# Graph layer with a feed-forward network on one core: 32x32 block transposes on VectorE in place of TensorE's, down products one tile later, zeros on ScalarE's queue

## The chip, the cores and the metric

The kernel runs on 1 core of one Trainium2 chip. The metric is the device time of one execution in microseconds. Before the change it is 1678.12 us, the median of three runs.

## The reference

2500 nodes with 1024 features, 42500 edges. `xn` is the layer norm of `x`.

```
x = x + segment_sum((xn @ W)[src] * edge_weight, dst) + mix(xn)
x = x + ffn(layernorm(x))

mix:  q, k = xn @ Wq.T + bq, xn @ Wk.T + bk     (16 heads of 64), each divided by its norm
      s = sum over the map of phi(q) * phi(k);  v = xn @ Wv.T + bv;  out = s * v / s
ffn:  gate = silu(bitlinear(x, w_gate)); up = bitlinear(x, w_up); bitlinear(gate * up, w_down)
      bitlinear: rows scaled to integers of -128..127 by their largest value,
                 weights to -1, 0, 1 by their mean absolute value, then x @ w.T  (inner size 512)
```

## The kernel before

Rows are handled in 20 tiles of 125. Each engine has a program written out by hand, and semaphores order them; the order on an engine is the order of its code. Products in near full precision split both operands into a high part (made by ScalarE) and a low part (made by VectorE) and take three matmuls, `product3` at L364. The stages follow each other on TensorE:

- Gram stage (to about 163 us): rows are normalised, transposed and stored to `xnT`, and TensorE makes products of all rows, `gram` at L1391. Meanwhile GpSimd writes zeros into a dense matrix, `A_dense`, one strip of 1.28 MB at a time.
- Weight stage (to 313): high and low parts of Wq and Wk (`high_of_weights`, `low_of_weights`), then `fold`, which makes the map weights.
- Map stage (to 546): `map_tile`, 48 matmuls per tile with TH and TL. VectorE's `ex` add at L1144 starts when TensorE has ended the tile. VectorE also works off the edges in pairs of columns, `edges`, after the numbers of EDGE_PLAN, and GpSimd adds them into the dense matrices by indirect DMAs, `scatter_pair`: the first 20 pairs (ALONE) into matrix 0, each after a strip of zeros of matrix 1, the rest in turn into both. In tiles 10 to 17 a block of 128 rows of Wv is transposed by TensorE (`transposes`, eight matmuls against `ident`), copied back by ScalarE (L848) and stored by SP (L522).
- Stage of W (to 769): `source_tile`, results S stay in SBUF.
- Value stage (to 992): the same with Wv in WH and WL. VectorE's four steps after a tile are in `stage4_tile` (L1173 to L1180). Tiles 6 to 17 also take a chunk of the feed-forward weights each: VectorE scales and rounds it, ScalarE makes bf16 of it (L884), TensorE transposes it (L1569), ScalarE copies it (L887), SP stores it to `ternary` (L600).
- Aggregation (to 1553): five groups of four output tiles (eight PSUM banks). For each of the 20 source tiles ScalarE makes SH and AH, VectorE adds the two loads of the dense matrices and makes SL and AL (`low_of_sources`), TensorE does 24 matmuls of 512 columns. There are two buffers of each, so ScalarE's copy waits until TensorE has released that buffer. Between the pairs of source tiles VectorE quantises the four tiles of the group before, `quantise_r`; ScalarE's `integers` makes bf16 of each into `rq16`.
- FFN (to the end): `ffn_tile` on TensorE does gate and up (16 matmuls, L1645), transposes the hidden rows (four, L1658) and the quantised rows of the tile two later (eight, L1624), and the down products (eight, L1675). The last group's rows are normalised and quantised meanwhile, `largest_r` and `round_r`, at the tiles of ROUNDED_AT. `hidden` is VectorE's work on a tile's gate and up, `add_down` adds its down products.

Of the kernel before, what the change touches and what calls it, by code (L numbers as in the profile page):

```python
# [58 lines left out]
ALONE = 20  # L59
# [14 lines left out]
X_BANK = (0, 4)  # L74
# [7 lines left out]
EDGE_PLAN = [1] * TILES + [0, 0, 0, 0, 1, 1, 1, 1] + [0, 1, 1, 0, 1, 1, 0, 1] + [1, 0, 1, 0, 1, 0, 1, 1] \  # L82
    + [1, 1, 1, 1, 1, 1, 0, 0] + [4] + [2] * KT + [3] * (TILES - KT) + [4] * 18 + [0] * 2
# [20 lines left out]
def layer_kernel(nc, x, src, dst, edge_weight, W, Wq, bq, Wk, bk, Wv, bv, mix_w, w_gate, w_up, w_down, out):  # L104
# [8 lines left out]
    wT_d = nc.dram_tensor("ternary", (12, P, D), BF16).ap()  # L113

# [116 lines left out]
    rq16 = e3("rq16", [P, TILES, D], BF16)  # L231
# [4 lines left out]
    rqT = s6("rqT", [P, 2, KT, P], BF16)  # L236
# [29 lines left out]
    s_acc = sems("s_acc", GT)  # L266
# [129 lines left out]

    PAIRS_OF = (ALONE + (BLOCKS * PAIRS - ALONE) // 2, (BLOCKS * PAIRS - ALONE) // 2)

    def wait_stage4(eng):

        for i in range(2):
# [6 lines left out]
            eng.wait_ge(s_fout[i], 16 * 6)  # L408
# [4 lines left out]
    V_LOAD, V_TURN = KT, KT + 2  # L413

# [24 lines left out]
    def _(sp):  # L439
# [141 lines left out]
        def stage4_tile(h, i, chunk):  # L581
# [13 lines left out]
            if chunk is not None:  # L595
# [1133 lines left out]
```

## Time and profile before

| | |
|---|---|
| runs | 1686.17, 1676.09, 1678.12 us |
| profiled execution | 1680.37 us, of which the span is 1678.6 |
| granted clock of TensorE, mean | 0.998 |
| TensorE busy | 1653.2 us |
| VectorE busy | 1095.4 us |
| ScalarE busy | 519.1 us |
| GpSimd busy | 588.5 us |
| DMA | 302.93 MB, 180 GB/s over the span |

Busy time is the time in which the engine has an instruction under way. TensorE's matmuls overlap each other by part, so a mean of 380 ns for a matmul does not mean that one takes 380 ns of the engine's time; the distance between starts does.

### The profile page before, as it was taken

The numbers are of one execution on the slowest core, as the hardware profiler recorded it, in microseconds if no ns is written. First come the engines' busy times: TensorE is split into PE (matmuls) and PEld (weight loads), VectorE is DVE, ScalarE is ACT, GpSimd is POOL, SyncE is SP. The second block draws the span as 40 slices with busy tenths as digits, with TensorE's granted clock in tenths as the row PEclk, the third lists the DMA queues.
The fourth block names the chain that finished last, engine by engine and source line by source line (L and its number), as shares of the span: only waits on it lengthen the run. The fifth ranks groups of instructions, "written<-read, shape, count | busy, mean of one in ns | idle before, by whom it ended". The sixth has DMA issues, their size and how long they took to land.

```text
span 1678.6 us, 23146 instructions
## 1 busy us (share of the span) xinstructions
PE 1653.2 (98%) x8036; PEld 1344.9 (80%) x8036; DVE 1095.4 (65%) x2548; ACT 519.1 (31%) x618; POOL 588.5 (35%) x392
## 2 busy tenths in 40 slices
PE   6999999999999999999999999999999999999998
PEld 5899999888888888888877777888788887887665
DVE  7866573576676876656666664476485674764886
ACT  4632210222222111114232222233333333332554
POOL 2011565777776777777677700000000000000000
PEclk9999999999999999999999999999999999999999
DMA  9999878655676755657877747345345345452454
GB/s 295 377 402 348 308 234 263 169 138 124 151 195 167 183 141 149 149 138 191 243 209 192 191 147 205 102 135 137 96 146 136 96 136 145 136 145 62 146 172 123
DMA packets 158003, 302.93 MB, mean 180 GB/s; under 512 B 60241, under 2 KB 95105, under 8 KB 157938
## 3 DMA queue, kind: packets, MB, share of 16 engines
q1 hardware_dynamic: 88302, 222.54, 42.2%
q0 software_dynamic: 61824, 52.62, 15.3%
q10 hardware_dynamic: 7812, 26.97, 5.3%
q8 instruction: 32, 0.52, 0.1%
q14 instruction: 33, 0.27, 0.1%
HBM read 202.88 MB, written 99.20 MB: 180 GB/s over the span
## 4 chain that ended last, share of the span: by engine, by line
PE 91%; DMA 5%; DVE 2%; issue 1%; ACT 1%; SPq 0%; DVEq 0%; ACTq 0%
PE PS L367 23%; PE PS L368 23%; PE PS L366 23%; PE PS L1408 4%; PE PS L1410 4%; PE PS L1409 4%; PE PS L1645 4%; DMA Aside<-A_dense 2%; PE PS L1675 2%; PE PS L1472 2%; DMA xnT<-XT 1%; DMA X<-in_x 1%; PE PS L1624 1%; DVE stats L995 1%; PE PS L1388 0%
## 5 line engine op out<-in xcount | busy, mean ns | idle before, releaser
L706 POOL DMA_INDIRECT A_dense<-wtot,cell x336 | 545.4, 1623 | 229.5 <-DMA A_dense<-wtot,cell 133.9
L367 PE MATMUL PS<-SH,AL 125*125 125x512 f32 x784 | 310.0, 395 | 0.0
L366 PE MATMUL PS<-SL,AH 125*125 125x512 f32 x784 | 308.4, 393 | 1.6 <-DVE AL L1222 1.4
L368 PE MATMUL PS<-SH,AH 125*125 125x512 f32 x784 | 309.8, 395 | 0.0
L366 PE MATMUL PS<-WL,xtH 128*125 128x512 f32 x640 | 252.9, 395 | 0.0
L367 PE MATMUL PS<-WH,xtL 128*125 128x512 f32 x640 | 252.0, 394 | 0.0
L368 PE MATMUL PS<-WH,xtH 128*125 128x512 f32 x640 | 251.6, 393 | 0.0
L1220 DVE TENSOR_TENSOR SL<-S,SH 125x1024 fp32r<-125x1024 f32 x98 | 119.9, 1223 | 166.1 <-ACT SH L895 166.1
L895 ACT ACTIVATE SH<-S 125x1024 fp32r (+1 forms) x98 | 103.9, 1061 | 316.4 <-PE PS L368 316.3
L366 PEld LDWEIGHTS PS<-SL,AH 125*125 125x125 f32 x784 | 145.9, 186 | 39.8 <-DVE AL L1222 3.1
L367 PEld LDWEIGHTS PS<-SH,AL 125*125 125x125 f32 x784 | 146.1, 186 | 36.0
L368 PEld LDWEIGHTS PS<-SH,AH 125*125 125x125 f32 x784 | 145.5, 186 | 34.5
L378 DVE SCALAR_TENSOR_TENSOR junk<-keyrow,key,ewrow 128x256 bf16<-128x256 f32 x336 | 149.0, 480 | 2.1 <-DMA ewrow<-weight_rows 1.8
L368 PEld LDWEIGHTS PS<-WH,xtH 128*125 128x125 f32 x640 | 118.9, 186 | 28.8
L366 PEld LDWEIGHTS PS<-WL,xtH 128*125 128x125 f32 x640 | 118.9, 186 | 28.4
L367 PEld LDWEIGHTS PS<-WH,xtL 128*125 128x125 f32 x640 | 119.0, 186 | 28.0
L366 PE MATMUL PS<-TL,xtH 128*125 128x512 f32 x320 | 126.7, 396 | 0.0
L367 PE MATMUL PS<-TH,xtL 128*125 128x512 f32 x320 | 126.7, 396 | 0.0
L368 PE MATMUL PS<-TH,xtH 128*125 128x512 f32 x320 | 126.2, 394 | 0.0
L1120 DVE TENSOR_TENSOR xtL<-xt,xtH 128x1000 fp32r<-128x1000 f32 x60 | 71.9, 1198 | 71.5 <-ACT xtH L826 71.2
L691 POOL DMA_DIRECT2D A_dense<-zeros x40 | 46.6, 1165 | 143.5 <-PE PS L1410 83.2
L1408 PE MATMUL PS<-ring 125*128 125x512 f32 (+4 forms) x260 | 90.3, 347 | 5.2 <-DVE ring L1012 5.2
(190 smaller groups left out, 2547.9 us busy)
## 6 DMA issues: line engine op xcount, KB each, us to landing
A_dense<-zeros POOLq DMA_DIRECT2D x40, 1280.0 KB, 8.3
xt<-xnT SPq DMA_DIRECT2D x60, 500.0 KB, 6.1
Araw<-A_dense SPq DMA_DIRECT2D x100, 250.0 KB, 2.7
Aside<-A_dense SPq DMA_DIRECT2D x100, 250.0 KB, 2.9
keyrow<-key_rows SPq DMA_DIRECT2D x42, 512.0 KB, 4.1
ewrow<-weight_rows SPq DMA_DIRECT2D x42, 512.0 KB, 5.6
xnT<-XT ACTq DMA_DIRECT2D x20, 500.0 KB, 10.2
zx<-in_x SPq DMA_DIRECT2D x20, 448.0 KB
```

Of the source, the lines that this page charges most:

```text
L366: nc.tensor.matmul(o, lh, rl, start=start, stop=False)
L367: nc.tensor.matmul(o, ll, rh, start=False, stop=False)
L368: return nc.tensor.matmul(o, lh, rh, start=False, stop=stop)
L378: nc.vector.scalar_tensor_tensor(junk[:, slot, 2 * c:2 * c + 2, :].rearrange("p a n -> p (a n)"), row, key[:, col], wrow, ALU.is_equal, AL ...
L706: pool.indirect_dma_start(cells[m], bass.IndirectOffsetOnAxis(cell[:, col:col + 1], 0), wtot[:, col:col + 1], None, compute_op=ALU.add).th ...
L895: nc.scalar.activation(sh, S[0:ROWS, bass.ds(s, 1), :].rearrange("p o n -> p (o n)"), ACT.Copy).then_inc(s_s[i], 1)
L1120: nc.vector.tensor_tensor(xtL[i][:, :, :], xt[:, i], xtH[i][:, :, :].bitcast(F32), ALU.subtract).then_inc(s_xtl[i], 1)
L1220: nc.vector.tensor_tensor(sl, S[0:ROWS, bass.ds(s, 1), :].rearrange("p o n -> p (o n)"), sh.bitcast(F32), ALU.subtract)
L1408: nc.tensor.matmul(o, hi[:, cols], rl, start=first and opens, stop=False, skip_group_check=True)
L1409: nc.tensor.matmul(o, lo[:, cols], rh, start=False, stop=False, skip_group_check=True)
L1410: last = nc.tensor.matmul(o, hi[:, cols], rh, start=False, stop=last_one, skip_group_check=True)
L1645: last = nc.tensor.matmul(PS[0:ROWS, 2 * i + c, :], rqT[:, i, k, 0:ROWS], wT[:, c, :, k * P:(k + 1) * P], start=k == 0, stop=k == KT - 1)
```

## The change

1. Wv: VectorE turns each 128 rows in 32x32 blocks from `stage` into `turned`, in the same tiles as before. Four stores per block of rows put the blocks in place in `wvT`. ScalarE and TensorE drop out. WH and WL are then filled by columns, so the last tile pair with W and the first with Wv go by column halves (`half_products`).
2. Feed-forward weights: VectorE turns the bf16 chunk after `stage4_tile`, SP stores it in eight parts after the tile's loads.
3. Quantised rows: ScalarE's integers go into one half of `rc`, VectorE turns them into the other (`turn_rows`), four stores put them into DRAM (`rqT_d`) and one load fetches the tile into `rqT`, both from ScalarE's queue in aggregation and from SP's for the last group. The buffer `rc` is free again when the stores have landed. TensorE takes its weights from `rqT` with a step of eight elements.
4. FFN: no transposes of quantised rows; the down products of a tile follow gate and up of the second next tile; the transposed hidden rows have two banks.
5. Zeros of matrix 1 are written from ScalarE's queue with the high parts of Wq and Wk; ALONE is 12; three empty scatters are left out; four edge pairs move from the map stage to the weight stage.

```diff
-ALONE = 20
+ALONE = 12
+COLS = FULL + 1
...
-EDGE_PLAN = [1] * TILES + [0, 0, 0, 0, 1, 1, 1, 1] + [0, 1, 1, 0, 1, 1, 0, 1] + [1, 0, 1, 0, 1, 0, 1, 1] \
-    + [1, 1, 1, 1, 1, 1, 0, 0] + [4] + [2] * KT + [3] * (TILES - KT) + [4] * 18 + [0] * 2
+EDGE_PLAN = [1] * TILES + [0, 0, 0, 0, 1, 1, 1, 1] + [0, 1, 1, 1, 1, 1, 0, 1] + [1] * KT \
+    + [1, 1, 1, 1, 1, 1, 0, 0] + [4] + [2] * KT + [3, 3] + [3, 2] * (KT // 2) + [3, 3] + [4] * 18 + [0] * 2
...
-    rq16 = e3("rq16", [P, TILES, D], BF16)
+    rqT = e3("rqT", [P, TILES, D], BF16)
...
+    def zero_strip(eng, m, r, sem):
+        eng.dma_start(A[m][r * P:(r + 1) * P, :].rearrange("p (r c) -> p r c", r=5),
+                      zeros[:, None, :].to_broadcast([P, 5, A_PITCH // 5])).then_inc(sem, 16)
...
+    def turn_blocks(out_, in_):
+        order_in, order_out = across_blocks(in_)
+        return nc.vector.transpose(order_out(out_), order_in)
+
+    def store_turned(eng, dram, rows, sem):
+        for a in range(4):
+            eng.dma_start(dram.rearrange("(b i) (a f) -> a i b f", b=4, a=4)[a],
+                          rows[a * 32:(a + 1) * 32, :].rearrange("p (b f) -> p b f", b=4)).then_inc(sem, 16)
+
+    def store_halves(eng, dram, rows, sem, down):
+        for a in range(4):
+            for c in range(2):
+                if down:
+                    to = dram.rearrange("(b i) (c a f) -> c a i b f", b=4, c=2, a=4)[c, a]
+                else:
+                    to = dram.rearrange("(b i) (a c f) -> c a i b f", b=4, c=2, a=4)[c, a]
+                eng.dma_start(to, rows[a * 32:(a + 1) * 32, :].rearrange("p (b c f) -> p b c f", b=4, c=2)[:, :, c]).then_inc(sem, 16)
 
     def wait_stage4(eng):
...
+    def integer_rows(i):
+        return rc[:, i, 0:D // 2].bitcast(BF16)
+
+    def turned_rows(i):
+        return rc[:, i, D // 2:D].bitcast(BF16)
+
+    def store_rows(eng, g, d):
+        eng.wait_ge(s_turn, g * GT + d + 1)
+        store_turned(eng, rqT_d[bass.ds(g * GT + d, 1)].rearrange("o p n -> (o p) n"), turned_rows(d % 2), s_rqst[d % 2])
+
+    def fetch_rows(eng, g, d):
+        eng.wait_ge(s_rqst[d % 2], 64 * (g * (GT // 2) + d // 2 + 1))
+        eng.dma_start(rqT[:, bass.ds(g * GT + d, 1), :].rearrange("p o n -> p (o n)"),
+                      rqT_d[bass.ds(g * GT + d, 1)].rearrange("o p n -> (o p) n")).then_inc(s_rqT[d % 2], 16)
 
...
-                sp.wait_ge(s_vev, j + 1)
-                sp.dma_start(wvT_d[:, :, j * P:(j + 1) * P].rearrange("k p n -> p k n"),
-                             by_block(stage[:, j % 2, :])).then_inc(s_vout, 16)
+                sp.wait_ge(s_vtr, j + 1)
+                store_turned(sp, wvT_d[j], turned[:, :], s_vout)
             j = t - V_LOAD
             if 0 <= j < KT:
                 sp.wait_ge(s_w2l, KT)
                 if j >= 2:
-                    sp.wait_ge(s_vout, 16 * (j - 1))
+                    sp.wait_ge(s_vtr, j - 1)
...
-                sp.wait_ge(s_fT[i], chunk // 2 + 1)
-                sp.dma_start(wT_d[chunk], fTb[:, i, :]).then_inc(s_fout[i], 16)
+            if chunk is not None:
+                sp.wait_ge(s_fT[i], chunk // 2 + 1)
+                store_halves(sp, wT_d[chunk], fTb[:, i, :], s_fout[i], chunk >= 8)
...
+            if n == 0:
+                act.wait_ge(s_const, 8)
+            for r in range(n * STRIPS // (2 * KT), (n + 1) * STRIPS // (2 * KT)):
+                zero_strip(act, 1, r, s_Bzero)
...
+                if d >= 1:
+                    store_rows(act, g - 1, d - 1)
                 integers(g - 1, d)
+                if d >= 2:
+                    fetch_rows(act, g - 1, d - 2)
...
-                act.wait_ge(s_ftr[i], h - 2)
-                act.wait_ge(s_fout[i], (h - 3) * 16)
-                nc.scalar.activation(fTb[:, i, :], PS16[:, 6 + i, :], ACT.Copy).then_inc(s_fT[i], 1)
...
+            j = t - V_TURN
+            if 0 <= j < KT:
+                dve.wait_ge(s_stage[j % 2], 32 + 16 * (KT // 2) + 16 * (j // 2) + 16)
+                if j:
+                    dve.wait_ge(s_vout, 64 * j)
+                turn_blocks(turned[:, :], stage[:, j % 2, :]).then_inc(s_vtr, 1)
...
+                dve.wait_ge(s_fq16[i], h - 2)
+                dve.wait_ge(s_fout[i], (h - 3) * 128)
+                turn_blocks(fTb[:, i, :], fqb[:, i, :]).then_inc(s_fT[i], 1)
...
-            dve.wait_ge(s_rq16[i], g * (GT // 2) + d // 2)
+            dve.wait_ge(s_rqst[i], 64 * (g * (GT // 2) + d // 2))
...
+        def turn_rows(g, d):
+            dve.wait_ge(s_rq16[d % 2], g * (GT // 2) + d // 2 + 1)
+            nc.vector.transpose(turned_rows(d % 2).rearrange("p (b j k) -> p b k j", b=4, j=32),
+                                integer_rows(d % 2).rearrange("p (k b j) -> p b k j", b=4, j=32)).then_inc(s_turn, 1)
...
+                turn_rows(g - 1, d)
...
+            hidden(t)
+            if t >= 2:
+                add_down(t - 2)
+            if t - 1 in ROUNDED_AT:
+                turn_rows(GROUPS - 1, ROUNDED_AT.index(t - 1))
...
+        def half_products(i, c):
+            cols = slice(c * 512, (c + 1) * 512)
+            for k in range(KT):
+                last = product3(PS[0:ROWS, 2 * i + c, :], xtH[i][:, k, :], xtL[i][:, k, :], WH[:, k, cols], WL[:, k, cols],
+                                k == 0, k == KT - 1)
+            return last
...
-                for e in range(8):
-                    last = nc.tensor.transpose(PS16[:, 6 + i, e * P:(e + 1) * P], fqb[:, i, e * P:(e + 1) * P], ident16[:, :])
-                last.then_inc(s_ftr[i], 1)
...
+            rows = rqT[:, bass.ds(m * 2 + i, 1), :].rearrange("p o (r k) -> p (o r) k", k=KT)
+            pe.wait_ge(s_rqT[i], 16 * m + 16)
             pe.wait_ge(s_h[i], m)
...
-                    last = nc.tensor.matmul(PS[0:ROWS, 2 * i + c, :], rqT[:, i, k, 0:ROWS], wT[:, c, :, k * P:(k + 1) * P],
+                    last = nc.tensor.matmul(PS[:, 2 * i + c, :], rows[:, :, k], up_blocks(c, k),
...
+            gate_up(0, h)
+            transpose_hidden(h - 1, 1)
+            pe.wait_ge(s_z[1], HALF + h - 1)
+            down(h - 1, 0, 4, False)
+            gate_up(1, h)
+            transpose_hidden(h, 0)
+            pe.wait_ge(s_z[0], HALF + h)
+            down(h - 1, 1, 4, False)
```

ScalarE, in the group loop of aggregation, one quantising step before: SH and AH are the parts of a source tile, and `rq_131` is the integers' tile.

```order
L895 ACTIVATE SH<-S 125x1024
L898 ACTIVATE AH_127<-Araw 125x500
L910 REGISTER_ALU
L911 ISA
L911 ACTIVATE rq_131<-rc,neg_round 125x1024
L895 ACTIVATE SH<-S 125x1024
```

And now; the DMAs `rqT<-rc` are the stores of the tile before, four of them, and `rqT<-rqT` is the load of the tile before that one.

```order
L953 ACTIVATE SH<-S 125x1024
L956 ACTIVATE AH_128<-Araw 125x500
L465 REGISTER_ALU
L424 ISA
L424 DMA rqT<-rc 32x4x256
...
L968 REGISTER_ALU
L969 ACTIVATE rc<-rc,neg_round 125x1024
L469 REGISTER_ALU
L470 ISA
L470 DMA rqT<-rqT 128x1024
L953 ACTIVATE SH<-S 125x1024
```

The stores stand between a source tile's parts and the integers, and the load behind the integers.

VectorE, the same place before: the low part of the second source tile, then the next quantisation.

```order
L1215 TENSOR_TENSOR Araw<-Araw,Aside 125x500
L1220 TENSOR_TENSOR SL<-S,SH 125x1024
L1222 TENSOR_TENSOR AL_129<-Araw,AH_127 125x500
L1266 TENSOR_SCALAR rc<-zr,group_mv,rstd 125x1024
L1268 REGISTER_ALU
L1269 TENSOR_REDUCE f_sc<-rc 125x1
```

And now:

```order
L1288 TENSOR_TENSOR Araw<-Araw,Aside 125x500
L1293 TENSOR_TENSOR SL<-S,SH 125x1024
L1295 TENSOR_TENSOR AL_130<-Araw,AH_128 125x500
L1359 REGISTER_ALU
L1360 STREAM_TRANSPOSE rc<-rc 128x4x8x32
L1339 TENSOR_SCALAR rc<-zr,group_mv,rstd 125x1024
L1341 REGISTER_ALU
L1342 TENSOR_REDUCE f_sc<-rc 125x1
```

The transpose of the integers comes between the low part and the next quantisation.

TensorE, one FFN tile before: gate and up in two parts around the transposes of the hidden rows, then the transposes of quantised rows, then down.

```order
L1645 MATMUL PS<-wT,rqT 125x512 x12
L1658 MATMUL PS<-ident_50,hq_136 128x125 x4
L1645 MATMUL PS<-wT,rqT 125x512 x4
L1624 MATMUL PS<-ident_50,rq_131 128x125 x8
L1675 MATMUL PS<-wT,hqT 125x512 x8
```

And now, the end of a tile's 16 gate and up products and what follows them:

```order
L1703 MATMUL PS<-wT,rqT 128x512 x9
L1711 REGISTER_ALU
L1713 MATMUL PS<-ident_50,hq_136 128x125 x4
L1718 REGISTER_ALU
L1721 MATMUL PS<-wT,hqT 125x512 x8
```

The eight transposes of quantised rows are gone, and the hidden rows are transposed once gate and up of the next tile are complete.

## Rows read from the trace of the kernel before

**Rows 1.** The page, busy time (share of the span) and instructions of TensorE.

```profile
PE 1653.2 (98%) x8036; PEld 1344.9 (80%) x8036; DVE 1095.4 (65%) x2548; ACT 519.1 (31%) x618; POOL 588.5 (35%) x392
```

**Rows 2.** The page, the chain that ended last, share of the span by engine.

```profile
PE 91%; DMA 5%; DVE 2%; issue 1%; ACT 1%; SPq 0%; DVEq 0%; ACTq 0%
```

**Rows 3.** The chain in order of time, map stage (start us, us, what).

```profile
471.60 0.87 PE PS L1388 x8
```

**Rows 4.** Timeline of VectorE, value stage (start us, us, instruction, idle before).

```profile
958.15 1.23 DVE L1173 TENSOR_TENSOR PS<-PS,bvb 125x1024 f32<-125x1024 f32 x1 [3.92 <-PE PS L368]
...
969.72 1.23 DVE L1173 TENSOR_TENSOR PS<-PS,bvb 125x1024 f32<-125x1024 f32 x1 [3.74 <-PE PS L368]
```

**Rows 5.** Timeline of VectorE, map stage, one tile and the next one's start.

```profile
471.64 1.23 DVE L1144 TENSOR_TENSOR ex<-PS,bb 125x1024 f32<-125x1024 f32 x1 [2.76 <-PE PS L368]
...
478.87 1.19 DVE L1120 TENSOR_TENSOR xtL<-xt,xtH 128x1000 fp32r<-128x1000 f32 x1
483.65 1.23 DVE L1144 TENSOR_TENSOR ex<-PS,bb 125x1024 f32<-125x1024 f32 x1 [3.60 <-PE PS L368]
```

**Rows 6.** Timeline of TensorE's weight loads, one FFN tile.

```profile
1593.19 2.51 PEld L1645 LDWEIGHTS PS<-wT,rqT 128*125 128x125 bf16 x12
1595.78 0.43 PEld L1658 LDWEIGHTS PS<-ident,hq 125*128 125x128 bf16 x4
...
1599.04 2.51 PEld L1645 LDWEIGHTS PS<-wT,rqT 128*125 128x125 bf16 x12
```

**Rows 7.** Timeline of VectorE, FFN, tiles with the largest value and the rounding.

```profile
1589.72 0.80 DVE L1266 TENSOR_SCALAR rc<-zr,group_mv,rstd 125x1024 f32<-125x1024 f32 x1
...
1591.70 0.74 DVE L1319 SCALAR_TENSOR_TENSOR hid<-PS,u_back,gate 125x512 f32<-125x512 f32 x1
...
1594.51 1.28 DVE L1345 SCALAR_TENSOR_TENSOR fin<-PS,h_sc,rt 125x1024 f32<-125x1024 f32 x1
...
1595.70 0.14 DVE L1276 TENSOR_SCALAR x_back<-f_sc 125x1 f32<-125x1 f32 x1
...
1597.58 0.75 DVE L1319 SCALAR_TENSOR_TENSOR hid<-PS,u_back,gate 125x512 f32<-125x512 f32 x1
```

**Rows 8.** Timeline of TensorE, start of aggregation.

```profile
997.55 0.47 PE L366 MATMUL PS<-SL_first,AH 125*125 125x512 f32 x1 [1.02 <-DVE zx L1180]
```

**Rows 9.** Timeline of VectorE, aggregation, a quantising pair.

```profile
1254.25 0.81 DVE L1266 TENSOR_SCALAR rc<-zr,group_mv,rstd 125x1024 f32<-125x1024 f32 x1
...
1258.34 0.67 DVE L1215 TENSOR_TENSOR Araw<-Araw,Aside 125x500 f32<-125x500 f32 x1
...
1260.06 0.67 DVE L1222 TENSOR_TENSOR AL<-Araw,AH 125x500 fp32r<-125x500 f32 x1
...
1265.38 0.81 DVE L1266 TENSOR_SCALAR rc<-zr,group_mv,rstd 125x1024 f32<-125x1024 f32 x1
```

**Rows 10.** Timeline of ScalarE and its queue, the same pair and the next.

```profile
1262.56 1.06 ACT L895 ACTIVATE SH<-S 125x1024 fp32r<-125x1024 f32 x1 [2.89 <-PE PS L368]
...
1264.03 1.14 ACT L911 ACTIVATE rq<-rc,neg_round 125x1024 f32 x1
...
1273.68 1.06 ACT L895 ACTIVATE SH<-S 125x1024 fp32r<-125x1024 f32 x1 [2.89 <-PE PS L368]
1274.19 0.35 ACTq L100 DMA_DIRECT2D zr<-z  x1
...
1274.71 0.40 ACTq L101 DMA_DIRECT2D zr<-z  x1
```

**Rows 11.** Landing of a strip of zeros, a slow issue, ScalarE's high parts of Wq and Wk.

```profile
A_dense<-zeros POOLq DMA_DIRECT2D x40, 1280.0 KB, 8.3
...
8.71 7.63 SPq L460 DMA_DIRECT2D brows<-in_L_mix_bq  x1
...
L796 ACT ACTIVATE split<-raw x16: 1045/1064/1136, 164.1 to 227.4; 128x1026 fp32r<-128x1026 f32 x16
```

**Rows 12.** Groups of weight loads by form, FFN (busy us, mean ns).

```profile
L1645 PEld LDWEIGHTS PS<-wT,rqT 128*125 128x125 bf16 x320 | 42.4, 138 | 22.0
```

More of the change, by code:

```diff
@@ L542, in _ @@
             if t == 17:
-                for i in range(2):
-                    sp.wait_ge(s_Azero[i], 16 * A_PITCH // P)
+                zeros_written(sp)
                 for j in range(2, 7):
@@ L703, in scatter_pair @@
             turns[m] += 1
-            for c in range(2):
-                col = 2 * pair + c
+            for col in range(2 * pair, min(2 * pair + 2, COLS)):
+                c = col % 2
                 pool.indirect_dma_start(cells[m], bass.IndirectOffsetOnAxis(cell[:, col:col + 1], 0),
@@ L1180, in stage4_tile @@
             nc.vector.tensor_tensor(zx[0:ROWS, i, :], v, zx[0:ROWS, i, :], ALU.add).then_inc(s_z[i], 1)
-        with dve.Fori(0, 2) as h:
-            for i in range(2):
-                low_of_tile(1 - i, h + 2 * HALF + i)
-                stage4_tile(h, i)
+        stage4_tile(0, 0)
+        low_of_tile(0, 1 + 2 * HALF)
+        stage4_tile(0, 1)
+        for i in range(2):
+            low_of_tile(1 - i, 1 + 2 * HALF + i)
+            stage4_tile(1, i)
         low_of_tile(1, 2 + 2 * HALF)
@@ L1309, in scales_back, with hidden @@
                                     ALU.mult).then_inc(s_fb, 1)
[L1311 to L1314 removed]
+        def hidden(t):
+            h, i = divmod(t, 2)
+            sc, hh = h_sc[0:ROWS, t % 3, :], hid[0:ROWS, i, :]
             n = t * 5
@@ L1358, in _ @@
         dve.wait_ge(s_fb, 1)
-        hidden(0, 0)
+        hidden(0)
         row_stats(GROUPS - 1, ORDER[2:])
@@ L1373, in _ @@
         dve.wait_ge(s_fb, 2)
-        for t in range(TILES - GT - 2, TILES - 2):
-            hidden(t // 2, t % 2)
-            add_down(t - 1)
-        hidden(HALF - 1, 0)
-        hidden(HALF - 1, 1, 2)
+        for t in range(TILES - GT - 2, TILES - 1):
+            hidden(t)
+            add_down(t - 2)
+        hidden(TILES - 1)
         for t, bank in ((TILES - 3, 4), (TILES - 2, 0), (TILES - 1, 2)):
@@ L1509, in tile_products @@
                                     wl[:, k, cols], k == 0, k == KT - 1)
-                if used is not None and k + 1 < KT:
-                    last.then_inc(used, 1)
             last.then_inc(s_mm[i], 1)
@@ L1546, in _ @@
             pe.wait_ge(s_supev[i], HALF - 1)
-            source_tile(HALF - 1, i, used=s_wk if i else None)
+            pe.wait_ge(s_xtl[i], HALF + PASS)
+            last = half_products(i, 0)
+        last.then_inc(s_wk, 1)
+        for i in range(2):
+            half_products(i, 1).then_inc(s_mm[i], 1)
+        pe.wait_ge(s_vl, KT // 2)
         for i in range(2):
@@ L1551, in _ @@
             pe.wait_ge(s_supev[i], HALF)
-            tile_products(i, WH, WL, ready=s_vl if i == 0 else None)
+            half_products(i, 0)
+        pe.wait_ge(s_vl, KT)
+        for i in range(2):
+            half_products(i, 1).then_inc(s_mm[i], 1)
         with pe.Fori(1, 3) as h:
@@ L1598, in sources, with aggregate @@
                     last.then_inc(s_acc[d], 1)
-                if ends and d == ORDER[2]:
-                    for n in range(2):
-                        pe.wait_ge(s_rq16[n], (TILES - GT) // 2)
-                    pe.wait_ge(s_r[ORDER[0]], GROUPS)
-                    rows_across(0, 0, X_BANK[0])
             last.then_inc(s_pe5[i], 1)
-        def aggregate(g, ends=False):
+        def aggregate(g):
             for i in range(2):
```

260 lines of the change are left out of this document (109 added, 151 removed).

## The prediction

> **What bounds the kernel now.** I read the page's busy lines first: TensorE is busy for 1653.2 of 1678.6 us [rows 1]; then the chain that ended last, which is TensorE for 91% [rows 2]. So an instruction taken off TensorE shortens the run by the time that it holds TensorE, until another engine ends later than TensorE would. Then I went through the timelines of each stage for what stands ready how early. The sum is made against the profiled execution's 1680.37 us (span 1678.6), which is 2.2 us above the median of 1678.12; it is carried to the median at the end.
>
> **What leaves TensorE.** (a) 64 transposes of Wv, eight in each of eight tiles of the map stage: each eight is 0.87 us of the chain [rows 3]. 8 x 0.87 = 7.0 us. (b) 96 transposes of the ternary weights, eight in each of twelve tiles of the value stage. VectorE's first step of a tile starts when TensorE ends the tile, and two such starts are 11.57 us apart [rows 4]; a map tile with the same 48 products takes 12.01 - 0.87 = 11.14 [rows 3, 5]. 12 x 0.43 = 5.2 us. (c) 160 transposes of the quantised rows. An FFN tile goes from 1593.19 to 1599.04, 5.85 us; its first twelve products take 2.59, 0.216 each [rows 6], so 24 take 5.19, and the twelve transposes the other 0.66, 0.055 each. Eight of them go: 20 x 0.44 = 8.8 us. The gain if everything else keeps up is 21.0 us.
>
> **What VectorE gets.** 40 block transposes of 128x1024; the trace has none. A pass over as many elements with one input in the fast form takes 0.80 us [rows 7], the low part of a tile, two inputs and 1000 elements, 1.19 [rows 5]. I take 1.2, because a transpose has to take the elements one by one as that pass does, and keep 0.8 and two such passes, 2.4, as ends.
>
> **Where it is hidden.** Map stage: from the start of its first step VectorE ends the next tile's low part after 8.4 us (471.64 to 478.87 + 1.19) with three edge pairs in between [rows 5]. With 1.2 more that is 9.6 of 11.14: no charge, and none up to a transpose of 2.7. Value stage: VectorE waits 3.7 to 3.9 us for TensorE in each such tile [rows 4], and the transpose lies in that gap. SP issues eight small stores instead of one, some 0.4 us each, ahead of the next tile's load; that load comes 3 us later, and the low part that needs it now stands ready before the gap of 3.7 us begins. No charge for the twelve tiles. But the first loads of A stand behind the last eight stores and behind their landing, about 6 us later than now. TensorE stalls 1.0 us there for the last tile's sum [rows 8], and VectorE, which does the late A tiles first, would give that sum later: +2 us (0 to 4). At its start the value stage takes tiles 0 and 1 by column halves, so both end close together and the low part of tile 2 stands behind the four steps of tile 0: +1 us (0 to 2).
>
> **Aggregation.** This gives most back. A pair of source tiles takes TensorE 11.12 us, from one release to the next, 1262.56 to 1273.68 [rows 10]. In a quantising pair VectorE quantises for 4.1 us (1254.25 to 1258.34), has source 0 ready at 1260.7 [rows 9], then waits for ScalarE's copy of source 1, which starts when TensorE releases that buffer at 1262.56 [rows 10] and starts on source 0. So 1.83 us are free. At 1265.38, 2.8 us after the release, the next quantisation begins [rows 9]. The change puts a transpose between, and it needs ScalarE's integers. They ended at 1265.17 [rows 10]. From the second pair on ScalarE's sequencer issues four stores ahead of them. Two issues stand 0.52 us apart, and they start while the engine still works on what was queued before: the copy starts at 1273.68, the first issue is at 1274.19 [rows 10]. So four issues run from 0.5 to 2.6 after the release, the integers from 2.7 to 3.85, the transpose from 3.95 to 5.15. That is 2.35 us more on VectorE against 1.83 free: 0.5 us late. The next quantisation in the same buffer also waits until the stores have landed, some 2 to 3.5 us after the last issue: +0.3. So 0.8 us for each of two pairs, nearly nothing for the first, which has no stores before it, and the fourth transpose has no quantisation behind it. Per group 1.5 us; four groups, +6 us. A transpose of 0.8 with stores that don't hold the integers makes it 1 us, one of 2.4 makes it 20.
>
> **FFN.** The new order gives TensorE 5.19 + 4 x 0.055 = 5.41 us a tile. VectorE needs 2.81 for the hidden rows (1591.70 to 1594.51) and 1.19 for the sum, 1.98 in a tile with the largest value (1589.72 to 1591.70), 1.88 in one with the rounding (1595.70 to 1597.58) [rows 7], and 1.2 for a transpose. Over tiles 3 to 13 that is 11 x 4.0 + 4 x 5.06 = 64.2 us against TensorE's 59.5: VectorE becomes the bound there. It may lag 1.7 us before TensorE waits: 5.41 less the 2.8 of the hidden rows and about 0.9 for ScalarE's pass over them, an estimate from its copy of twice as many elements, 1.06 [rows 10], and two hand-overs. What is left is 64.2 - 59.5 - 1.7 = +3 us. Today it needs 59.4 of TensorE's 64.4 there. Down products a tile later cover the sum, not this: the hidden rows are what VectorE owes first. The waits at the stage's start stay, they come from the last group's statistics.
>
> **The zeros.** ScalarE's queue issues the 20 strips of the second matrix with the high parts of Wq and Wk, 164 to 228 us; a strip takes 8.3 us to land [rows 11], so they pile up, and an issue can block: one of SP's in the first microseconds, with many behind it, took 7.6 us [rows 11]. The second weight's high parts are made while TensorE still multiplies the first's, so half of the items have time to spare. +1.5 us (0 to 8). The scatters start on two matrices earlier and so end earlier; but the first A loads come after their end today already, so this frees nothing on the path.
>
> **Sum.** -7.0 - 5.2 - 8.8 + 2 + 1 + 6 + 3 + 1.5 = -7.5 us: 1672.9 on the profiled run, 1670.6 on the median; I say 1670.
>
> **Strided weight loads.** The FFN's weight loads step by eight bf16 elements where they read 125 neighbours in 138 ns [rows 12]; products follow every 216, so 78 ns are free. No row shows a strided load. At the bound of twice the row, 276 ns, 320 x 0.060 = +19 us; I take 0, since the load would have to slow 1.6 times before TensorE feels it.
> The Trainium skill, SBUF — State Buffer, in its note on SBUF cachelines, says that accesses to one 16-byte line run at full bandwidth, that each access which crosses to a new line pays a penalty, and yet that eight bf16 elements may be stepped for free. By the last part the sum stays; by the middle part this rival comes out. No run shows which.
>
> **Rivals.**
> - All of it hidden: a transpose of 0.8 and stores that overlap leave some 2 us of stalls: -19, 1659 us. For it: the charges are sums of small overruns, each within what a row can mislead. Against: VectorE's free time lies outside the quantising pairs. 0.2.
> - The other side: a block transpose takes 2.4 us, two passes. Each microsecond over 1.2 costs twelve times in aggregation (three of four transposes in four groups) and four in the FFN, 16 in all; the gain is gone at 0.47 over, from a transpose of 1.67 us on. At 2.4: 1670 + 19 = 1689. For it: its write steps by eight elements and nothing in the trace is like it. 0.12.
> The Trainium skill, VectorE: DVE Perf Modes, section The three transpose paths, has 311 ns for 128x128 in bf16; eight of those, an estimate, are 2.5 us, as in this rival, if none of it is a fixed cost.
> - Strided weight loads at 276 ns: 1670 + 19 = 1689. 0.1.
> - ScalarE's queue blocks on the zeros so long that the gram stage starves: 1677. 0.06.
> - It doesn't do what it says, the transposes having run in gaps of TensorE: rows 3 speak against it. 0.02.
> - The forecast: 0.5.
>
> **How the numbers follow.** A measurement here can tell about 1% (16.8 us). Faster by more, below 1661.3: the hidden case and a little of the forecast's lower edge, 0.22. Slower by more, above 1694.9: two of the slow cases together, or one at worse than its price, 0.12. Between: 0.66. The range takes in the hidden case and each slow one at its price: 1657 to 1691, with 0.1 outside on either side.
>
> **What the profile after would show.** Map tiles 11.14 us apart throughout, value tiles the same; a transpose near 1.2 us on VectorE; in aggregation TensorE waiting 0.5 to 1 us for VectorE's low parts, twice in each of four groups; FFN tiles 5.4 us apart at the end and up to 6 in tiles 4 to 13, with waits for ScalarE's integers; weight loads of 138 ns. I would be wrong through a transpose far from 1.2, stores that don't delay the integers, or a weight load over 216.

## The result and the profile after

The change makes the kernel slower: 1743.4 us (median of four, 1738.94 to 1747.7) against 1677.11 before, a ratio of 1.0382, 95% interval 1.0340 to 1.0423. I had said 1670. The profiled execution has a span of 1746.0 us.

The page after: busy time by engine, and the chain that ended last. They answer to [rows 1, 2].

```profile
PE 1656.6 (95%) x7716; PEld 1338.4 (77%) x7716; DVE 1211.1 (69%) x2589; ACT 480.9 (28%) x578; POOL 557.3 (32%) x369
...
PE 59%; DVE 18%; DMA 10%; issue 6%; ACT 2%; SPq 2%; ACTq 2%; DVEq 0%
```

TensorE has 320 matmuls fewer and is as busy as before, and the chain has left it for two fifths of the span. Two things can do that, waits and a lower clock, and both are there. The stages, each from its first matmul to that of the next, from the traces (us):

| kernel | ratio to before (95%) | to map | map | W and values | aggregation | FFN | span |
|---|---|---|---|---|---|---|---|
| before | | 312.8 | 229.8 | 449.6 | 561.0 | 125.4 | 1678.6 |
| changed | 1.0382 (1.0340 to 1.0423) | 318.7 | 222.8 | 452.3 | 616.6 | 135.6 | 1746.0 |
| e1_turn_view | 1.0065 (1.0048 to 1.0082) | 319.1 | 222.8 | 448.1 | 568.6 | 122.0 | 1680.6 |
| e4_turn_view_4 | 1.0158 (1.0129 to 1.0187) | 318.9 | 222.8 | 449.7 | 578.6 | 126.4 | 1696.4 |
| s1_step_1 | 1.0201 (1.0159 to 1.0243) | 322.0 | 222.8 | 450.9 | 596.4 | 122.1 | 1714.2 |
| s2_step_2 | 1.0066 (1.0043 to 1.0089) | 322.1 | 222.8 | 449.6 | 571.1 | 122.1 | 1687.7 |
| s2z_zeros_pool | 1.0013 (1.0003 to 1.0023) | 311.6 | 222.8 | 447.0 | 569.3 | 122.0 | 1672.7 |
| s2zl_load_first | 0.9991 (0.9977 to 1.0004) | 310.9 | 222.8 | 449.8 | 570.6 | 122.2 | 1676.3 |
| s2zi_integers_first | 0.9972 (0.9956 to 0.9987) | 311.2 | 222.8 | 450.5 | 565.4 | 122.1 | 1672.0 |
| sbest_all | 0.9978 (0.9963 to 0.9993) | 312.0 | 222.8 | 450.4 | 568.4 | 122.2 | 1675.8 |
| k12_weights_only | 0.9985 (0.9972 to 0.9998) | 309.9 | 222.8 | 450.3 | 566.5 | 125.4 | 1674.9 |
| k12l_load_first | 0.9966 (0.9954 to 0.9979) | 311.2 | 222.8 | 448.5 | 561.5 | 125.4 | 1669.4 |
| k12f_tile_3_early | 0.9965 (0.9952 to 0.9979) | 310.8 | 222.8 | 447.8 | 562.3 | 125.4 | 1669.1 |

The ratios come from all executions of a kernel, the stages from one traced execution. A stage differs by up to 4 us between kernels that are alike there (W and values take 452.3, 448.1 and 449.7 us in the changed kernel, e1_turn_view and e4_turn_view_4, which run the same program up to there), so only larger differences are read from it. And the traced execution can lie off the median: it is 7.0 us below it in e1_turn_view, 4.7 in e4_turn_view_4 and 6.1 in s2z_zeros_pool, and 4.3 above it in the changed kernel. In the changed kernel, 55.6 of the 67.4 us more are in aggregation. The groups by form show why (busy us, mean ns of one):

```profile
L1360 DVE STREAM_TRANSPOSE rc<-rc 128x1024 bf16<-128x1024 bf16 x20 | 96.5, 4823 | 20.6 <-ACT rc L969 20.5
L420 DVE STREAM_TRANSPOSE fTb<-fqb 128x1024 bf16<-128x1024 bf16 x12 | 14.8, 1234 | 0.0
L420 DVE STREAM_TRANSPOSE turned<-stage 128x1024 f32<-128x1024 f32 x8 | 9.9, 1234 | 0.0
L367 PE MATMUL PS<-SL,AH 125*125 125x512 f32 x784 | 316.8, 404 | 36.4 <-DVE AL L1295 36.4
L1703 PEld LDWEIGHTS PS<-wT,rqT 128*128 x288 | 41.4, 144 | 20.8 <-issue 0.2
```

The same operation on the same number of bf16 elements takes 1.234 us for the weights and 4.823 for the quantised rows. TensorE waits 36.4 us for low parts. VectorE in the second quantising pair of the first group (start us, us) shows how; it answers to [rows 9]:

```profile
1137.04 4.84 DVE L1360 STREAM_TRANSPOSE rc<-rc 128x1024 bf16<-128x1024 bf16 x1
1141.50 0.89 DVE L1339 TENSOR_SCALAR rc<-zr,group_mv,rstd 125x1024 f32<-125x1024 f32 x1
...
1147.39 0.67 DVE L1295 TENSOR_TENSOR AL<-Araw,AH 125x500 fp32r<-125x500 f32 x1
...
1152.79 4.82 DVE L1360 STREAM_TRANSPOSE rc<-rc 128x1024 bf16<-128x1024 bf16 x1 [2.41 <-ACT rc L969]
```

TensorE's timeline has the other end of that wait, just behind VectorE's low part:

```profile
1148.12 0.79 PE L367 MATMUL PS<-SL,AH 125*125 125x512 f32 x1 [4.38 <-DVE AL L1295]
```

Two stretches of the span around and behind it, of 20 us and of 1 (columns: stretch, its length, busy time of PE, PEld, DVE, ACT, POOL, then TensorE's granted clock, DMA share, GB/s):

```profile
1143.80:1163.80 20.00, 13.92 (x48) 10.72 (x48) 17.00 (x21) 5.96 (x7) 0.00 (x0) 0.83 0.23 65
...
1151.00:1152.00 1.00, 1.00 (x4) 0.80 (x3) 0.00 (x0) 0.39 (x1) 0.00 (x0) 0.50 1.13 328
```

After a wait of 4.4 us TensorE works, but at the lower of its two clock levels, 1.2 GHz: its products follow each other every 0.43 us until 1153.4, and every 0.23 from there on. Apart from the one at its very end, the trace has ten such falls, 47.8 us long together, and the trace of before only one of 3.4 us; eight of the ten, 41 us, lie in aggregation, each beside a wait of 3.6 to 4.4 us. 5 of the 41 us fall into the waits themselves; half of the other 36 is given away, 18 us. In e1_turn_view (below) aggregation has no fall, TensorE waits 6.4 us there for low parts instead of 36.4, and 1.5 instead of 3.6 for the last value tile's sum. So waits make 30 + 2 and the clock 18 us of the difference, 50 for a measured 48.

### The profile page after: what moved, and what is told of

Its sections match the earlier page's. It is cut to its first block, busy times and chain, and to the rows that moved or that the text cites. A ratio compares the mean times of both kernels' runs of the same rounds, so it can differ in the third digit from the quotient of the medians.

```text
span 1746.0 us, 22716 instructions
## 1 busy us (share of the span) xinstructions
PE 1656.6 (95%) x7716; PEld 1338.4 (77%) x7716; DVE 1211.1 (69%) x2589; ACT 480.9 (28%) x578; POOL 557.3 (32%) x369
## 3 DMA queue, kind: packets, MB, share of 16 engines
q0 software_dynamic: 54672, 26.41, 10.4%
## 4 chain that ended last, share of the span: by engine, by line
PE 59%; DVE 18%; DMA 10%; issue 6%; ACT 2%; SPq 2%; ACTq 2%; DVEq 0%
PE PS L367 15%; PE PS L368 15%; PE PS L369 15%; PE PS L1490 3%; PE PS L1492 3%; PE PS L1491 3%; DMA Aside<-A_dense 3%; DMA z<-zx 3%; DVE SL L1293 2%; PE PS L1554 2%; DVE rc L1360 1%; DVE stats L1316 1%; DVE Araw L1288 1%; DMA xnT<-XT 1%; DVE AL L1295 1%
## 5 line engine op out<-in xcount | busy, mean ns | idle before, releaser
L758 POOL DMA_INDIRECT A_dense<-wtot,cell x333 | 532.7, 1600 | 256.3 <-DMA A_dense<-wtot,cell 145.7
L367 PE MATMUL PS<-SL,AH 125*125 125x512 f32 x784 | 316.8, 404 | 36.4 <-DVE AL L1295 36.4
L368 PE MATMUL PS<-SH,AL 125*125 125x512 f32 x784 | 316.2, 403 | 0.0
L369 PE MATMUL PS<-SH,AH 125*125 125x512 f32 x784 | 315.5, 402 | 0.0
L367 PEld LDWEIGHTS PS<-SL,AH 125*125 125x125 f32 x784 | 149.9, 191 | 79.7 <-DVE AL L1295 42.0
L953 ACT ACTIVATE SH<-S 125x1024 fp32r<-125x1024 f32 (+1 forms) x98 | 103.7, 1059 | 292.1 <-PE PS L369 292.1
L368 PEld LDWEIGHTS PS<-SH,AL 125*125 125x125 f32 x784 | 150.5, 192 | 36.9
L369 PEld LDWEIGHTS PS<-SH,AH 125*125 125x125 f32 x784 | 149.6, 191 | 36.2
L1360 DVE STREAM_TRANSPOSE rc<-rc 128x1024 bf16<-128x1024 bf16 x20 | 96.5, 4823 | 20.6 <-ACT rc L969 20.5
L882 ACT ACTIVATE xtH<-xt 128x1000 fp32r<-128x1000 f32 x60 | 61.9, 1032 | 133.9 <-DMA xt<-xnT 133.9
## 6 DMA issues: line engine op xcount, KB each, us to landing
A_dense<-zeros POOLq DMA_DIRECT2D x20, 1280.0 KB, 10.5
```

What stands on the lines that cost most here:

```text
L367: nc.tensor.matmul(o, lh, rl, start=start, stop=False)
L368: nc.tensor.matmul(o, ll, rh, start=False, stop=False)
L369: return nc.tensor.matmul(o, lh, rh, start=False, stop=stop)
L758: pool.indirect_dma_start(cells[m], bass.IndirectOffsetOnAxis(cell[:, col:col + 1], 0), wtot[:, col:col + 1], None, compute_op=ALU.add).th ...
L882: nc.scalar.activation(xtH[i][:, :, :], xt[:, i], ACT.Copy).then_inc(s_xth[i], 1)
L953: nc.scalar.activation(sh, S[0:ROWS, bass.ds(s, 1), :].rearrange("p o n -> p (o n)"), ACT.Copy).then_inc(s_s[i], 1)
```

## Experiments

**e1_turn_view** takes away the difference in how the two transposes write: where neighbours are put.

```diff
-    nc.vector.transpose(turned_rows(d % 2).rearrange("p (b j k) -> p b k j", b=4, j=32),
+    nc.vector.transpose(turned_rows(d % 2).rearrange("p (b k j) -> p b k j", b=4, j=32),
```

> The changed kernel with one edit: the transposes of the quantised rows write each block's 32 neighbours side by side, as those of the ternary weights do (1.23 us), where the changed kernel writes them 16 bytes apart (4.82 us). Stores, loads and weight loads are left as they are, so the quantised rows' elements land in other places and the feed-forward results are not the reference's. Theory A (the write step alone makes 4.82 of 1.23, and the long transpose causes the waits): the transpose takes 1.2 us, aggregation falls from 617 to about 565 us, the FFN from 136 to about 120, the whole from 1743 to about 1677 (1668 to 1690). Rival B (the transpose is slow because source and destination lie in one buffer, or because of where it runs): it stays near 4.8 us and the time near 1743. Rival C (the stores queued ahead of ScalarE's integers, and their landing, cause the waits): the transpose falls to 1.2 us, but aggregation keeps over half of its 55 us and the whole stays over 1710.

It took 1689.31 us, and the transpose 1.244. Theory A holds, with aggregation at 568.6 (expected 565); B and C fall. The same groups as above:

```profile
L1360 DVE STREAM_TRANSPOSE rc<-rc 128x1024 bf16<-128x1024 bf16 x20 | 24.9, 1244 | 16.6 <-ACT rc L969 16.6
L367 PE MATMUL PS<-SL,AH 125*125 125x512 f32 x784 | 309.1, 394 | 6.5 <-DVE AL L1295 6.4
```

The whole came out 12 us above the 1677 expected, at the upper end of the range. Some 5 of them are in the trace (1682.34 us), where aggregation lies 3.6 us and the FFN 2 above what I expected. The first 319 us kept the 6 that they had lost, as nothing in this edit touches them. The other three executions took 1688.9 to 1690.2 us with a mean granted clock of 0.993 to 0.995, where the traced one had 0.998. They left no trace, so where their 7 us lie is not shown. s2_step_2 (below), traced at 1689.42 us and 0.994, has four clock falls ahead of its end, 17.1 us together: one in the weight stage, one in the value stage, two in aggregation.

**p1_steps** measures the disputed cost by itself. Each added operation is like this one, with another step s:

```diff
+    nc.vector.transpose(turned_rows(0).rearrange("p (q j s) -> p q s j", j=32, s=8),
+                        integer_rows(0).rearrange("p (q s j) -> p q s j", j=32, s=8)).then_inc(s_probe, 1)
```

> The kernel of e1_turn_view (feed-forward results not the reference's) with thirteen added operations of VectorE on zeros ahead of the second group of aggregation, each waiting for the one before: transposes of 128x1024 bf16 that write with a step of 1, 2, 4, 8, 16 and 32 elements, one that reads with a step of 8 and writes with 1, transposes of 128x512 fp32 with steps of 1, 2, 4 and 8, and plain copies of 128x1024 bf16 with steps of 8 and 1. Theory by lines of 16 bytes: 1.2 us at steps 1 and 2, about 2.4 at 4, 4.8 at 8 and no more at 16 and 32; fp32 at its full price from step 4 on. Rival by any step: 4.8 from step 2 on. Rival by bytes spanned: it goes on growing at 16 and 32. If the price belongs to strided writes and not to the transpose, the copy with step 8 is slower than the one with step 1 too. The time of the whole is of no use here.

Timeline of VectorE; in order: bf16 writes with a step of 1, 2, 4, 8, 16 and 32 elements, a read with a step of 8, fp32 with 1, 2, 4 and 8, and copies with 8 and 1.

```profile
1110.15 1.25 DVE L1371 STREAM_TRANSPOSE rc<-rc 128x1024 bf16<-128x1024 bf16 x1
1111.43 1.35 DVE L1374 STREAM_TRANSPOSE rc<-rc 128x1024 bf16<-128x1024 bf16 x1
1112.81 2.50 DVE L1377 STREAM_TRANSPOSE rc<-rc 128x1024 bf16<-128x1024 bf16 x1
1115.34 4.71 DVE L1380 STREAM_TRANSPOSE rc<-rc 128x1024 bf16<-128x1024 bf16 x1
1120.09 4.45 DVE L1383 STREAM_TRANSPOSE rc<-rc 128x1024 bf16<-128x1024 bf16 x1
1124.57 4.62 DVE L1386 STREAM_TRANSPOSE rc<-rc 128x1024 bf16<-128x1024 bf16 x1
1129.22 1.97 DVE L1389 STREAM_TRANSPOSE rc<-rc 128x1024 bf16<-128x1024 bf16 x1
1131.23 0.71 DVE L1392 STREAM_TRANSPOSE rc<-rc 128x512 f32<-128x512 f32 x1
1131.97 0.71 DVE L1395 STREAM_TRANSPOSE rc<-rc 128x512 f32<-128x512 f32 x1
1132.72 1.08 DVE L1398 STREAM_TRANSPOSE rc<-rc 128x512 f32<-128x512 f32 x1
1133.83 1.10 DVE L1401 STREAM_TRANSPOSE rc<-rc 128x512 f32<-128x512 f32 x1
1134.96 2.43 DVE L1404 COPY rc<-rc 128x1024 bf16<-128x1024 bf16 x1
1137.43 0.43 DVE L1407 COPY rc<-rc 128x1024 bf16<-128x1024 bf16 x1
```

The price of bf16 writes doubles from a step of 4 bytes to one of 8 and again to 16, and is flat from there. That is what the theory by lines of 16 bytes forecast for bf16; the rival by any step and the one by bytes spanned fall. It is not the transpose alone that pays: the copy goes from 0.43 to 2.43. Part of that may be the loss of a faster form that the dense copy has (0.42 ns an element, where the dense transpose takes 1.2); no run separates the two. A read with a step of 16 bytes pays far less (1.97). And the theory does not carry over to fp32: with 8 bytes between writes, two in a line, fp32 pays nothing (0.71) where bf16 pays double, and with 16 bytes it adds 0.37 us for 512 elements, 0.7 ns each, where bf16 adds 3.4 ns each (1.25 to 4.71 for 1024). So the price by step is measured, and the lines behind it are not shown.

**s1_step_1 and s2_step_2** compute the reference with a narrower step. The loads put neighbours back in order, four where there was one, and TensorE reads its weights with the same step:

```diff
-    nc.vector.transpose(turned_rows(d % 2).rearrange("p (b j k) -> p b k j", b=4, j=32),
-                        integer_rows(d % 2).rearrange("p (k b j) -> p b k j", b=4, j=32))
+    nc.vector.transpose(turned_rows(d % 2).rearrange("p (b q j s) -> p b q s j", b=4, j=32, s=STEP),
+                        integer_rows(d % 2).rearrange("p (q s b j) -> p b q s j", b=4, j=32, s=STEP))
...
+    for a in range(4):
+        eng.dma_start(rqT[...].rearrange("p o (q a f) -> p a (o q) f", a=4, f=32 * STEP)[:, a],
+                      rqT_d[...].rearrange("o p (a q f) -> (o p) a q f", a=4, f=32 * STEP)[:, a])
```

> The changed kernel with the quantised rows turned into a layout that keeps neighbours side by side all the way (step 1), so that weight loads read 128 neighbours; four loads per tile in runs of 64 bytes fetch it where one load did. Computes the reference. Theory A: the transpose takes 1.2 us and the whole lands near 1677, some us more if the four loads with short runs hold ScalarE's queue (1670 to 1695). Rival B: transpose near 4.8, time near 1743. Rival C: over 1710.

> The same with a step of two bf16 elements (4 bytes) between neighbours, in runs of 128 bytes. Computes the reference. If the price comes from each write that leaves the 16-byte line of the one before it, four of them share a line here and the transpose stays near 1.2 us (up to 1.9); if any step other than one costs the whole price, it takes 4.8 us and the time is near 1743.

s2_step_2 took 1689.96 us with transposes of 1.335: as e1_turn_view. s1_step_1, which differs from it in nothing but the step and the length of the runs, took 1714.35, above its range. The transpose is 1.243, but the four loads of 64-byte runs hold ScalarE's queue for 4.36 us, where those of 128-byte runs in s2_step_2 hold it for 2.15 (at 1274.91 us). The next copy stands behind them (ACTq is the queue, "issue" a wait for it):

```profile
1284.92 4.36 ACTq L472 DMA_DIRECT2D rqT<-rqT  x4
1289.33 1.06 ACT L955 ACTIVATE SH<-S 125x1024 fp32r<-125x1024 f32 x1 [3.49 <-issue]
```

**e4_turn_view_4** puts a third point between 1.24 and 4.82 us. Its edit is that of s2_step_2's transpose alone, with s=4.

> As e1_turn_view (stores, loads and weight loads as in the changed kernel, feed-forward results not the reference's), but the transposes of the quantised rows write with a step of four elements, 8 bytes: 2.5 us by the row of p1_steps, between 1.24 of e1_turn_view and 4.82 of the changed kernel. The prediction priced each microsecond over 1.2 at 16 us of the whole. By that slope: 1689 + 16 x 1.25 = 1709 us. If the price is flat up to some cover and steep behind it: under 1700. If the clock's falls after a stall (eight stretches in the aggregation of the changed kernel) start only with long stalls, the first step costs less than the second: from 1.24 to 2.5 under 16 us per us, from 2.5 to 4.8 over it.

The transpose took 2.502 us, the whole 1702.85 (1698.17 to 1710.15). From 1.24 to 2.50 a microsecond costs 10.8 of the medians (12.6 of the spans), from 2.50 to 4.82 it costs 17.5 (21.4). That is the order of the third theory, but the times alone do not settle it: by the ratios with their intervals the two are 12 ± 5 and 16 ± 4 us for each microsecond.

The clock speaks for it. Over four executions each, the granted clock is 0.995 on average in e1_turn_view, 0.995 in e4_turn_view_4 and 0.985 in the changed kernel. The share that is missing, taken of the time, is 8, 8 and 27 us, an estimate: nothing of the first step and 18 of the 41 us of the second. The mean alone is a weak measure (one execution of before has 0.949 at an ordinary 1682.02 us), but the traces agree: TensorE's waits in aggregation stay at 2.1 us or less in e4_turn_view_4, with no clock fall there; in the changed kernel they reach 4.4, with eight. But no sharp line shows: s2_step_2 has three falls behind waits of 1.8 to 2.3 us, and one wait of 3.6 us in the changed kernel (it ends at 1001.8 us) has none.

**s2z_zeros_pool** moves the zeros.

```diff
-    for r in range(n * STRIPS // (2 * KT), (n + 1) * STRIPS // (2 * KT)):
-        zero_strip(act, 1, r, s_Bzero)
...
+    for r in range(STRIPS):
+        zero_strip(pool, 1, r, s_Bzero)
+        if r < ALONE:
+            scatter_pair(r)
```

> s2_step_2 with the zeros of matrix 1 issued from GpSimd's queue, among its first scatters, in place of ScalarE's. In the changed kernel the weight stage is 9 us longer than before, and ScalarE's queue stands in an issue for 7.7, 4.0 and 3.8 us there. Theory Q (those blocked issues hold back the high parts): the map stage starts near 313 us where it starts at 322 in s2_step_2, and the whole falls from 1690 to about 1682. Rival E (the four edge pairs that VectorE does more in the weight stage hold it): the map stage starts at 320 or later and the time stays within 2 us of 1690.

Theory Q holds: the map stage starts at 311.6 instead of 322.1, the whole took 1680.51 (the traced execution 1674.45). ScalarE and its queue in the changed kernel: the last two high parts of Wq start at 187.5 and 192.7 us, where before the change all eight were done by 180.2.

```profile
178.77 8.70 ACTq L407 DMA_DIRECT2D A_dense<-zeros  x1
187.52 1.06 ACT L848 ACTIVATE split<-raw 128x1026 fp32r<-128x1026 f32 x1 [7.70 <-issue]
187.54 5.06 ACTq L407 DMA_DIRECT2D A_dense<-zeros  x1
192.65 1.06 ACT L848 ACTIVATE split<-raw 128x1026 fp32r<-128x1026 f32 x1 [4.07 <-issue]
```

**s2zi_integers_first** swaps two statements in ScalarE's loop.

```diff
-    if d >= 1:
-        store_rows(act, g - 1, d - 1)
     integers(g - 1, d)
+    if d >= 1:
+        store_rows(act, g - 1, d - 1)
```

> s2z_zeros_pool with ScalarE's integers put ahead of the four stores of the tile before, in aggregation. In e1_turn_view the three issues that stand behind the copies hold the integers from 1255.2 to 1256.5 us, and VectorE waits 1.2 us for them before the transpose. If that wait is what is left of aggregation's excess (569.3 us against 561.0 before), aggregation falls to 562 to 564 and the whole by 5 to 7 us, to 1674 or 1675. If the transpose and the landing of the stores make the rest, it falls by under 2 us.

1673.66 us: 6.9 us less than s2z_zeros_pool against the runs of before beside each (1.0013 to 0.9972), with intervals well apart. Aggregation is 565.4 where it was 569.3, not the 562 to 564 expected, so 4 us over the 561.0 of before stay. VectorE's timeline names what is late next: the transpose now follows the low part at once, and the next quantisation waits for the stores to land (0.87 us here).

```profile
1250.13 1.34 DVE L1360 STREAM_TRANSPOSE rc<-rc 128x1024 bf16<-128x1024 bf16 x1
1252.34 0.82 DVE L1339 TENSOR_SCALAR rc<-zr,group_mv,rstd 125x1024 f32<-125x1024 f32 x1 [0.87 <-DMA rqT<-rc]
```

**s2zl_load_first and k12l_load_first** put the eight stores of a chunk behind the next load on SP's queue (`store_chunk(chunk - 1)` behind `load_tile`).

> s2z_zeros_pool with SP's eight stores of a ternary chunk put behind the load of the next tile but one, where the changed kernel has them ahead of it. Theory L (the stores hold back that load, and with it the low part and VectorE's four steps): the stages of W and of the values, together 449.6 us in s2_step_2 and 452.3 in the changed kernel, take 445 to 446, and the whole falls by 3 to 4 us. Rival V (VectorE itself is full there with the transposes): no change over 1 us.

> k12_weights_only with the stores of a ternary chunk behind the load, as in s2zl_load_first. Theory L: 3 to 4 us less than k12_weights_only, about 1667, which is 0.6% under the kernel before. Rival V: as k12_weights_only.

Both medians fell by about 3 us (1680.51 to 1677.33, 1674.67 to 1672.02), with intervals that still overlap a little. But the stages do not show it where theory L has it: 447.0 to 449.8 in one pair, 450.3 to 448.5 in the other, and in these four traces the tiles from the seventh on are 11.0 or 11.1 us apart but for the last, and three before it in k12_weights_only (11.3, 12.0, 10.1). The changed kernel has four of 11.8 to 12.3. Where the 3 us come from is open, and sbest_all (below), which has this mend and that of s2zi_integers_first, is no faster than s2zi_integers_first alone (0.9978 and 0.9972), so whether they are there at all is open too.

**k12_weights_only** leaves parts 3 and 4 out.

> Parts 1 and 2 alone: Wv and the ternary weights are turned by VectorE; the quantised rows are transposed by TensorE and the FFN's order is that of before; the zeros are on GpSimd's queue. If part 3 is a loss even with a cheap transpose (aggregation 571 and FFN 122 us in s2_step_2 against 561 and 125.4 before, 7 us), this is faster than s2z_zeros_pool by 7 us and faster than before by 5 to 9 us: map stage 222.8 us, W and values 448 to 450, aggregation 561, FFN 125: about 1671. If part 3 pays its way, it is no faster than s2z_zeros_pool.

1674.67 us, 3.7 above the expectation, and 5.8 under s2z_zeros_pool, with intervals apart (0.9972 to 0.9998, 1.0003 to 1.0023): with a cheap transpose and the stores ahead of the integers, parts 3 and 4 still cost more than they gave.

**k12f_tile_3_early and sbest_all** issue the load of the value stage's tile 3 right behind that of tile 2.

> k12l_load_first with the load of the value stage's tile 3 issued right behind that of tile 2, ahead of SP's wait for tile 0's sum. In k12l_load_first tiles 1 to 6 are 11.3 to 13.4 us apart where the later ones are 11.05, and VectorE waits 5 to 6 us for each load: the load of tile 3 is issued at 783.0 us although its buffer was free at 759. If the late load starts that chain, tiles 1 to 6 come 11.1 us apart, and the whole falls by 3 to 4 us to about 1668. If VectorE's work at the start (two tiles' steps and two low parts in one) makes it, the spacing stays.

> All parts of the change with what the runs so far mend: rows turned with a step of two elements, zeros on GpSimd's queue, integers ahead of the stores, chunk stores behind the load, tile 3's load early. Computes the reference. Against k12f_tile_3_early it tells what part 3 and 4 are worth at their best: aggregation 563 and FFN 122 against 561 and 125.4, so within 2 us of it, about 1668. If part 3 still holds VectorE in aggregation, it is 5 us or more slower.

1671.35 us, no other than k12l_load_first: tiles 2 to 6 stay 11.5 to 12.7 us apart, so the late load does not start that chain. sbest_all took 1674.91, 3.6 us over k12f_tile_3_early where within 2 was expected (0.13% by the ratios, the intervals overlapping): with everything mended parts 3 and 4 are worth nothing or a little less. The best version is k12l_load_first or k12f_tile_3_early, 0.35% under the kernel before (0.21 to 0.48).

## Why the prediction was wrong

**The step that failed** is the price of the block transpose, "I take 1.2, because a transpose has to take the elements one by one as that pass does, and keep 0.8 and two such passes, 2.4, as ends". The 1.2 is exact for a dense write (1.234) and wrong by four for this one. All the rows I bounded it by write densely, and I called 2.4 the end although I had named the write with a step of eight elements as a reason for the slow case. I weighed what 16 bytes of step cost a weight load and not what they cost a write of VectorE. The way from there was right: the long transpose makes the low part late and TensorE waits for it, and e1_turn_view takes 48 of the 55.6 us away with the transpose alone. Slope 16 times 3.6 over 1.2 would have given 1670 + 58 = 1728, 15 short of 1743.4; e4_turn_view_4 puts the slope of the medians at 10.8 up to 2.50 us and at 17.5 beyond, where the clock falls come in.

Term by term, in e1_turn_view, where the transpose has the price I took:

- Gains. (a) -7.0 in the map stage: measured 229.8 to 222.8. (b) Later chunk tiles 11.0 or 11.1 us apart instead of 11.6, as forecast. (c) FFN tiles 5.41 apart at the end, as forecast. In the changed kernel's trace 7.0 stands, (b) is mostly lost.
- Value stage, +1 for its start and +2 for the A loads: W and values fell by 1.5 of the 5.2, so they cost 3.7. But the start costs more than said: tiles 2 to 6 come 60 us after tile 1 in five steps where 55 were due. In the changed kernel's trace the stage lost another 4 us, in four chunk tiles some 12 us apart. The load of the tile after next stands behind the eight stores on SP's queue, and SP got to them late: from 880 to 970 us it waited 5.0 us on average for the landing of a tile's results, against 3.1 in e1_turn_view, where the tiles keep their 11.0 or 11.1. The two kernels are the same up to there, so this is a difference between executions: "no charge for the twelve tiles" held in e1_turn_view and not here, and no run shows that the stores alone break it.
- Aggregation, +6: +7.6. The four issues ahead of the integers show as 1.2 us of VectorE's waiting a pair, the landing of the stores as 0.87 once that is gone; s2zi_integers_first took the first away for 4 us of aggregation and 7 of the whole.
- FFN, -8.8 + 3: -3.4. VectorE's tiles are 5.9 us apart in the middle, as forecast ("up to 6"). The gap to the sum is 2.4 us. In the changed kernel four tiles of 8.4 to 10.5 us hold a transpose each.
- Zeros, +1.5 (0 to 8): +5.9 at the start of the map stage, 10.5 between s2_step_2 and s2z_zeros_pool. The mechanism (an issue blocks) was right and my size too small: I said half of the items have time to spare, but the seventh and eighth high part of Wq, due at once, stood behind issues of 8.7 and 5.1 us.
- Strided weight loads, 0: right. They take 144 ns against 98 with a step of one (s1_step_1), under the 216 of a product.

These sum to 6.3 - 7.0 - 1.5 + 7.6 - 3.4 = +2.0, the difference of the spans, where I had -7.5 (the 6.3 are the zeros' 5.9 as this trace has them). The medians of e1_turn_view and of before are further apart, 10.4 us: the three executions without a trace are slower and had a lower clock, and no term of mine had that. So even at my price of a transpose the change would have been no gain; s2zi_integers_first shows what it takes to make it one.

**The rivals.** The slow transpose was the right one, at 0.12 and at half its real price: 2.4 us, where its own reason, the write with a step of eight, measured 4.82. What came on top, and no rival had, is the clock: long waits of TensorE made it lose time beside and after them too. The Trainium skill, SBUF — State Buffer, in its note on SBUF cachelines, has the penalty for each access that crosses to a new 16-byte line, and full bandwidth from two accesses per line on, hence eight bf16 elements for free. A penalty is what the runs show for bf16 writes; the free step is not: two elements per line already cost 2.50 against 1.25 us, one costs 4.71.

## What to carry to other kernels

Price an operation by its access pattern, not by its name: where neighbours in a VectorE write lie 8 or 16 bytes apart in bf16, look for a layout that keeps them within 4 bytes, and let the DMA's runs do the reordering (runs of 128 bytes cost nothing here, 1.0066 against 1.0065; runs of 64 bytes brought 24 us). When work moves from a full engine to one with free time, sum it within the stretch where it lands; a page's average (VectorE 65% busy) said yes where the quantising pairs had 1.83 us. And a wait of TensorE that grows to 3 or 4 us can cost more than itself: in the changed kernel's aggregation TensorE ran at half its clock beside or behind eight of the nine waits of 3.6 to 4.4 us.

## What the runs showed of the hardware

- VectorE's block transpose of 128x1024 takes 1.234 us in fp32 as in bf16, with dense writes.
- A weight load of 128 bf16 columns takes 98 ns with a step of one or two elements, where one of 125 columns takes 138 [rows 12]; with a step of eight it takes 144. The line is that of s1_step_1, a step of one:

```profile
L1705 PEld LDWEIGHTS PS<-wT,rqT 128*128 x288 | 28.2, 98 | 33.2 <-issue 0.2
```

The Trainium skill, TensorE: Matmul & The Clock Gate, section Weight-path perf modes — Fast Weight Load (FWL) and DoubleRow, has the fast form for 128 weights that are not fp32; by that rule, the traces agree at 98 and 138 ns, and show that a load with a step of eight takes no less than one of 125 columns.
- With strips of 1.28 MB issued close behind each other, one issue held ScalarE's queue for 8.7 us in the changed kernel.
